# Expert stage with stationary weights: up weights loaded per tile, gate weights copied per tile, four gather buffers

## The reference, cut to what matters

```python
E, K, H, F, R = (8, 2, 256, 512, 64)             # experts, chosen per token, width, hidden, rank
# x: 32 sequences of 64 steps, 256 wide = 2048 tokens
# 1 a gated recurrence over the 64 steps, 32 sequences at once
gate = sigmoid(h @ Wh.T + z_t @ Wz.T + b);  h = tanh(h * leak + gate * z_t)
# 2 a mixture of experts on its outputs
gate_hidden = einsum('nh,erh->ner', x, W_A)
scores = sqrt(sum(gate_hidden * gate_hidden, axis=-1))          # top 2 of 8, softmax of the two scores
g  = einsum('ner,efr->nef', gate_hidden, W_B)
up = einsum('nh,efh->nef', x, W_up)
y  = einsum('nef,ehf->neh', silu(g) * up, W_down)               # weighted by the two softmax weights
# 3 x = x + that; a second recurrence h = tanh(x_t @ Wx + b + h @ Wh); a quantised feed-forward; x = x + that
```

## Time and profile before

| | |
|---|---|
| median of 3 runs | 414.03 us (411.77 to 414.64) |
| profiled execution | 413.37 us |
| its span, first to last instruction | 411.6 us |
| PE, DVE, ACT, POOL busy, share of the span | 81%, 64%, 56%, 54% |
| stage A, expert stage, stage C, about | 0 to 129, 129 to 296, 296 to 411 us |

### The profile page before, as it was taken

The page is one execution under the profiler, slowest core; times in us unless marked ns, Lnnn a source line. Parts: engine busy times, 40 slices in busy tenths (PEclk is TensorE's granted clock), DMA queues, the critical chain, the costliest instruction groups (busy, mean ns, idle before and its releaser), DMA issues.

```text
span 411.6 us, 11966 instructions
## 1 busy us (share of the span) xinstructions
PE 332.1 (81%) x3816; PEld 229.1 (56%) x3817; DVE 265.0 (64%) x910; ACT 231.2 (56%) x730; POOL 223.1 (54%) x219
## 2 busy tenths in 40 slices
PE   2677777767836999899999798999947978888984
PEld 1444444444523667567666565666745756666852
DVE  6545565578844896685866686535345767768884
ACT  2356665655634554455554464455435766767982
POOL 5569999998973353545445455542033545454220
PEclk9999999996986999999999999999985899999999
DMA  8991357531231467522222232232221122121001
GB/s 220 231 369 41 100 221 280 203 118 40 78 96 32 150 177 210 167 84 76 70 82 74 72 86 70 70 77 51 66 65 53 28 66 66 51 76 51 29 27 52
DMA packets 24922, 42.97 MB, mean 104 GB/s; under 512 B 4066, under 2 KB 17762, under 8 KB 23988
## 3 DMA queue, kind: packets, MB, share of 16 engines
q1 hardware_dynamic: 19120, 23.50, 18.1%
q0 software_dynamic: 5488, 18.98, 15.8%
q10 hardware_dynamic: 276, 0.01, 0.0%
HBM read 28.97 MB, written 13.50 MB: 103 GB/s over the span
## 4 chain that ended last, share of the span: by engine, by line
PE 46%; another core or an unknown queue 8%; ACT 8%; DVE 5%; issue 3%; DMA 2%; POOL 1%; ACTq 0%; DVEq 0%; SPq 0%; POOLq 0%
PE bank L1036 12%; PE bank L1012 9%; PE bank L1024 4%; PE bank L999 3%; PE bank L830 3%; PE bank L1143 3%; PE bank L837 3%; PE bank L1173 2%; ACT z_hi L748 2%; PE bank L1107 2%; PE bank L990 1%; DMA gs<-gate_rows,row_of_slot 1%; ACT wrec L760 1%; PE bank L992 1%
## 5 line engine op out<-in xcount | busy, mean ns | idle before, releaser
L830 PE MATMUL bank<-h_hi,wrec_hi 128*128 128x32 f16 x512 | 43.9, 181 | 44.0 <-ACT h_hi L636 26.0
L830 PEld LDWEIGHTS bank<-h_hi,wrec_hi 128*128 128x128 f16 x512 | 34.0, 98 | 72.8 <-ACT h_hi L636 46.7
L536 POOL DMA_INDIRECT xs<-hs_rows,row_of_slot x37 | 35.2, 950 | 71.7 <-PE bank L992 58.3
L1036 PE MATMUL bank<-wdn_s,wrec 128*128 x468 | 59.9, 275 | 4.8 <-ACT wrec L678 3.7
L1012 PE MATMUL bank<-wup_s,xt 128*128 x234 | 62.9, 379 | 0.0
L1568 DVE TENSOR_TENSOR wrec<-bank,wrec 128x512 f16<-128x512 f32 x39 | 26.9, 690 | 47.7 <-ACT wrec L678 41.1
L1036 PEld LDWEIGHTS bank<-wdn_s,wrec 128*128 128x128 f16 x468 | 43.5, 97 | 24.3 <-issue 11.8
L560 POOL DMA_INDIRECT z_lo<-y_rows,slot_i x32 | 32.5, 1014 | 30.6 <-DVE stage L1682 16.0
L1298 DVE TENSOR_TENSOR_SCAN bank<-bank,terms 128x128 f32<-128x128 f32 x64 | 27.6, 431 | 27.7 <-ACT bank L632 25.8
L539 POOL DMA_INDIRECT gs<-gate_rows,row_of_slot x39 | 37.5, 961 | 11.9 <-issue 11.9
L672 ACT ACTIVATE z_lo<-bank 128x256 f32<-128x256 f32 x39 | 14.9, 383 | 49.7 <-PE bank L1036 37.3
(11 more groups left out here) (261 smaller groups left out, 969.1 us busy)
## 6 DMA issues: line engine op xcount, KB each, us to landing
y_rows<-z_lo SPq DMA_DIRECT2D x39, 128.0 KB
stage<-wup POOLq DMA_DIRECT2D x2, 2048.0 KB, 10.8
gate_rows<-ga_s SPq DMA_DIRECT2D x16, 256.0 KB, 3.2
stage<-wdn POOLq DMA_DIRECT2D x2, 2048.0 KB, 10.2
stage<-wb SPq DMA_DIRECT2D x2, 1024.0 KB, 13.2
hs_rows<-hs_out SPq DMA_DIRECT2D x16, 128.0 KB, 2.6
stage<-w SPq DMA_DIRECT2D x4, 512.0 KB
stage<-x_tm SPq DMA_DIRECT2D x4, 512.0 KB
```

The lines of the kernel that those rows point to most:

```text
L536: pool.indirect_dma_start(out=xs[par][:, :], out_offset=None, in_=hs_dram[0:tokens, :], in_offset=bass.IndirectOffsetOnAxis(ap=row_of_slot ...
L830: mm(fm(par)[:, ft, cols], w[:, m, kt, fcols], h_hi[pp][:, kt, pcols], start=False, stop=True, skip_group_check=True)
L1036: ins = mm(bank[6][:, 0:D], act_t[:, a, ft, :], w_slice(wdn_s, b, ft, e), start=n == 0, stop=n == len(todo) - 1)
```

## The change

- PE: in gate and up the weights become the stationary operand and the tokens move, in blocks of 128: gate has 8 matmuls of 128 columns (four of them over 64 rows), up has 24. The result comes out with the hidden dimension on partitions, so `transposed_act` is gone, and ACT and DVE split the activation straight from SBUF.
- The stationary weights lie at fixed places. Up: stage A writes the split weights to `expert_rows` in memory (`keep_weights`, four DMAs of 1 MB in 1 KB pieces, in SP's list behind tiles 6 to 9), and SP loads 512 KB per tile into one of four buffers that take the place of the high half of `wup_s`. Gate: ACT copies 128 by 512 f16 per tile (`gate_weights`); for tiles 0 and 1 SP copies them by DMA.
- Gate rows are stored twice side by side (512 B a row), by two DMAs whose pieces are 256 B; a gather brings 512 B. POOL's gathers have four buffers throughout and wait for the transposes of tile j-4.
- The two `split_rec` stand behind gathers 16 and 18. ACT stores the result of tile j-2 instead of j-1. Stage C's loads are 16 parts of 256 KB. The loops over tiles of PE and SP take four tiles at a time.

```diff
-    ga_dram = nc.dram_tensor("gate_rows", (NTOK * E, R), F32, kind="Internal").ap()
+    ga_dram = nc.dram_tensor("gate_rows", (NTOK * E, 2 * R), F32, kind="Internal").ap()
+    w_dram = nc.dram_tensor("expert_rows", (E * P, EXPERT_ROW), F16, kind="Internal").ap()
...
# SP
                 sp.wait_ge(ga_out, tile + 1)
-                sp.dma_start(ga_dram[bass.ds(tile * P * E, P * E), :].rearrange("(p e) c -> p (e c)", e=E),
-                             ga_s[par][:, :]).then_inc(ga_st[par], 16)
+                for c in range(2):
+                    sp.dma_start(ga_dram[bass.ds(tile * P * E, P * E), c * R:(c + 1) * R].rearrange("(p e) c -> p e c", e=E),
+                                 ga_s[par][:, :].rearrange("p (e c) -> p e c", e=E)).then_inc(ga_st[par], 16)
+            def keep_weights(n):
+                sp.wait_ge(w_split, n // 2 + 1)
+                kt, a = n // 2, n % 2
+                at = (a * KT + kt) * F
+                sp.dma_start(w_to[:, :, at:at + F], wup_s[:, a, kt]).then_inc(w_kept, 16)
+            def load_weights(j, b, of=None):
+                if live(j - 4, STILES):
+                    sp.wait_ge(u_mm, j - 3)
+                e = expert_of(j, of)
+                sp.dma_start(w_now[b], w_dram[bass.ds(e * P, P), :]).then_inc(w_here[b], 16)
+                return e
+            sp.wait_ge(w_kept, 16 * 4)
+            sp.wait_ge(s_word, 1)
+            for j in range(2):
+                e = load_weights(j, j)
+                sp.dma_start(gate_now[j][:, :], wb_s[:, bass.ds(e, 1), :].rearrange("p a f -> p (a f)")).then_inc(gate_first, 16)
+            store_gates(TILES - 2, 0)
+            load_weights(2, 2)
...
+            for j in range(16):
+                load_weights(j + 4, j % 4, min(j + 4, FIRST - 3) if j + 4 < FIRST else None)
                 store_y(j, j % 4)
                 load_part(j)
...
# POOL
-                    pool.wait_ge(xt_mm, (j - 3, j - 1)[j >= 6])
+                    pool.wait_ge(xt_mm, j - 3)
...
# ACT
+            def gate_weights(j, par):
+                sc.reg_load(word_reg, word_i[0:1, bass.ds(of, 1)])
+                e = sc.snap((packed >> 3 * (c + 1)) & (E - 1), min_val=0, max_val=E - 1)
+                sc.wait_ge(g_mm, j - 1)
+                sc.activation(gate_now[par][:, :], wb_s[:, bass.ds(e, 1), :].rearrange("p a f -> p (a f)"), ACT.Copy
+                              ).then_inc(gate_here, 1)
             def expert_tile(j, q):
                     silu_of(j, par)
+                    gate_weights(j + 2, par)
                     act_high(j - 1, 1 - par)
+                    store_tile(j - 2, (q - 2) % 4)
                     copy_in(j + 2, par)
-                    store_tile(j - 1, (q - 1) % 4)
...
# PE
-                ins = mm(bank[2][:, :], gh_s[par][:, :],
-                         wb_s[:, part, bass.ds(e, 1), :].rearrange("p a n -> p (a n)"), start=part == 0, stop=part == 1)
+            for f in range(FT):
+                mm(bank[2][:, block_of(f)], gate_now[par][:, block_of(f)], gh_s[par][:, :],
+                   start=f == 0, stop=False, skip_group_check=True)
+                ins = mm(bank[2][:, block_of(f)], gate_now[par][0:R, block_of(f)], gl_s[par][:, :],
+                         start=False, stop=True, skip_group_check=True)
...
+            for f in range(FT):
+                for n, (a, c) in enumerate(parts):
+                    ins = mm(bank[4 + par][:, block_of(f)], up_now[b][:, a, kt, block_of(f)], xt[par][:, c, kt, :], ...)
-            def transposed_act(j, par):
...
# DVE
-                ve.tensor_tensor(act_t[:, 1, :, :]..., bank[(7, 3)[par]][:, :], act_t[:, 0, :, :]..., ALU.subtract)
+                ve.tensor_tensor(act_t[par][:, 1, :, :]..., act[par][:, :], act_t[par][:, 0, :, :]..., ALU.subtract)
```

More of the change, by code:

```diff
@@ L36 @@
 ROUND = 1536.0
+EXPERT_ROW = 2 * KT * F
 def live(t, count=TILES):
@@ L104, in adaln_ffn @@
         wa_s = sb("wa_s", [P, 2, KT, E * R], F16)
-        wb_s = sb("wb_s", [P, 2, E, F], F16)
+        wb_s = sb("wb_s", [P, E, F], F16)
+        gate_now = [sb(f"gate_now{i}", [P, F], F16) for i in range(2)]
         wup_s = sb("wup_s", [P, 2, KT, E, F], F16)
@@ L171, in adaln_ffn @@
         x1t = free_w[:, 2 * F + 2 * D:2 * F + 3 * D].bitcast(F16).rearrange("p (a k t) -> p a k t", a=2, k=KT)
+        w_flat = wup_s[:, :, :, :, :].rearrange("p a k e f -> p (a k e f)")
+        w_now = [w_flat[:, b * EXPERT_ROW:(b + 1) * EXPERT_ROW] for b in range(4)]
+        up_now = [x.rearrange("p (a k f) -> p a k f", a=2, k=KT) for x in w_now]
         peak = sb("peak", [P, 4])
@@ L298, in adaln_ffn @@
         act_r = sem("act_r")
-        at_mm = sem("at_mm")
+        w_split = sem("w_split")
+        w_kept = sem("w_kept")
+        w_here = [sem(f"w_here{i}") for i in range(4)]
+        gate_first = sem("gate_first")
+        gate_here = sem("gate_here")
         at_hi_r = sem("at_hi_r")
@@ L383, in _ @@
+            w_to = w_dram.rearrange("(e p) n -> p e n", p=P)
+            def keep_weights(n):
[3 more added lines that the diff above has]
+                sp.dma_start(w_to[:, :, at:at + F], wup_s[:, a, kt]).then_inc(w_kept, 16)
             store_rows(0, 0)
-            with sp.Fori(0, (TILES - 2) // 2) as i:
+            for i in range((TILES - 2) // 2):
                 store_rows(2 * i + 1, 1)
                 store_gates(2 * i, 0)
+                if 3 <= i < 5:
+                    keep_weights(2 * i - 6)
@@ L497, in _ @@
             pool.wait_ge(s_stage[1], 32)
-            then_wait(split(wb_s[:, 0], wb_s[:, 1], stage[1][:, :].rearrange("p (e f) -> p e f", e=E)))
+            wb_f = stage[1][:, :].rearrange("p (e f) -> p e f", e=E)
+            then_wait(high(wb_s[:, :, :], wb_f))
+            then_wait(pool.tensor_tensor(wb_s[R:P, :, :], wb_f[R:P, :, :], wb_s[R:P, :, :], ALU.subtract))
             load_staged(3)
@@ L687, in copy_in @@
                               ).then_inc(xt_ready, 1)
-                sc.activation(gh_s[par][0:R, :], bank[0][0:R, 2 * P:3 * P], ACT.Copy).then_inc(gh_ready, 1)
+                sc.activation(gh_s[par][:, :], bank[0][:, 2 * P:3 * P], ACT.Copy).then_inc(gh_ready, 1)
             def silu_of(j, par):
@@ L740, in _ @@
             act_high(STILES - 1, 0)
+            store_tile(STILES - 2, (STILES - 2) % 4)
             def gelu(t, par, half):
@@ L1096, in _ @@
                        ).then_inc(position_mm, 1)
-            with pe.Fori(7, (STILES - 5) // 2) as i:
-                expert = experts()
-                expert_tile(2 * i + 3, 1, expert, 0)
-                expert_tile(2 * i + 4, 0, expert, 1, 2 * i + 5)
+            with pe.Fori(4, (STILES - 3) // 4) as i:
+                for q in (1, 3):
+                    expert = experts()
+                    expert_tile(4 * i + q, q, expert, 0)
+                    expert_tile(4 * i + q + 1, q + 1, expert, 1, 4 * i + q + 2)
             def x1_transposed(t, par):
@@ L1185, in tanh_tile @@
                     if isinstance(k, int) and (k, s) == (0, 0):
-                        down(STILES - 1, expert(1))
+                        down(STILES - 1, 0, expert(1))
                     if s == 0:
```

179 lines of the change are left out of this document (93 added, 86 removed).

## The result

The changed kernel is slower: 449.9 us (median, 447.0 to 450.8) against 413.2 us of the kernel before, run beside it, a ratio of 1.089 with a 95% interval of 1.085 to 1.094. Forecast were 397 us and a range up to 409. The profiled execution has a span of 449.0 us; stage A is as long as before, stage C within 2 us, and the whole loss lies in the expert stage.

A forecast was written before the change was run, and what follows sets the result against it. PE's columns were taken to set the expert stage's pace, with DVE a second bound in tiles 1 to 7. Terms -0.2 - 3.1 - 12.0 - 3.4 + 2.0 = -16.7 took 413.4 to 396.7, 397 against the median; forecast 391 to 401, range 387 to 409.

The forecast's parts named there:

- Transposes gone: Expert stage, PE: the f32 transposes of the activation fall away, saving 0.43 us of PE per tile.
- Gate and up in blocks: Expert stage, PE: 32 load and matmul pairs of 128 columns at 55 ns, 1.76 us against 1.73, +0.03 a tile.
- pace of the pairs: Rival, gate and up of every tile: at 98 ns a pair +54 us, so 450; chance 0.05.
- the columns stay: Gate and up on PE: the same 4096 columns as before, so the lower bound on added cost was nothing.
- The rule weighed there: Gate and up: about 81 ns per 128-column matmul in sustained pairs, 0.8 us more a tile, about 429 us.
- The gathers run four tiles ahead, which covers a late landing: Expert stage transfers: gathers issued early hide late landings; only tile 11's gather, in a fuller queue, was priced, +1 us.
- Tiles 0 to 9: Early expert stage: DVE's 25.3 us from tile 0's to tile 6's split becomes 22.2, giving -3.1 us.
- tiles 9 to 38: Rest of the expert stage: 30 tiles at 0.40 us less each, -12.0 us.
- late high halves: Expert stage, before down: ACT's high half comes about 1 us ahead, removing two thirds of 5.2 us short waits, -3.4.
- Start of the expert stage: Two weight loads and two gate copies land in time; without stage A's 5.7 us pause, about 2 us late.
- Stage A, ACT's copy, SP's list at nothing: Stage A's extra transfers and ACT's gate copy cost nothing; SP's waits there are already met; its expert-stage jitter shared +1 us.
- crowded stage A: Rival, stage A: 256 B gate pieces above 35 ns make stores late; 408 us at 41 ns; chance 0.06 beyond 44 ns.

The follow-up runs named there:

- e1: Changed kernel with the low gate product made over 128 rows, the lower 64 zero, instead of 64; on the quicker chip 375.3 us, ratio 0.999.
- e13: The kernel before, unchanged, traced again in a later batch: 412.3 us.
- e10: e7 with POOL's old wait, for the transposes of tile j-2 instead of j-4: 411.9 us, ratio 0.996 to the kernel before.
- e9: The kernel before with the run-ahead alone: four gather buffers throughout, POOL waiting for the transposes of tile j-4: 431.6 us, ratio 1.047.
- e18: The kernel before with a small POOL memset, not waited for, behind every indirect DMA: 407.0 us, ratio 0.986.
- e8: e1 with gate rows stored and gathered once, other half zero, so the product with the low gate weights is left out: 423.5 us, ratio 1.023.
- e6: The changed kernel, unchanged, run again in batch two on a chip of the 413 us: 446.9 us, ratio 1.078 to the kernel before.
- e7: e1 with the gate copies of tiles 0 and 1 issued earlier, behind the row store of tile 14: 425.4 us, ratio 1.028.
- e12: e7 again, unchanged, as the base of batch three: 425.1 us, ratio 1.030 to the kernel before.
- e11: e7 with weight loads of 128 rows of 128 B instead of 512 KB from tile 11 on, leaving out part of the computation: 425.9 us, ratio 1.031.

## Why the prediction was wrong

**Transposes gone, -0.43 a tile:** right; with equal shapes the tile is 3.44 us (e1), forecast 3.41.

**Gate and up in blocks, 55 ns a pair:** the step that failed. It held for up (56 ns) and was applied to the gate product too, whose matmuls alternate between 128 and 64 rows; the row behind it had only 128. Measured 160 ns, +0.84 us a tile: 4.27 instead of 3.41, and 3.44 in e1 where the shapes are equal. In time 21.5 us, on both kinds of chip. The rival "pace of the pairs" had the sign and the time (450), and decides from 68 ns on, but by luck: it put 98 ns on all 32 pairs, while up has 56 and the gate product 160, and over a third of the loss is the run-ahead's. Its reason, the pairs, is refuted by up. I spoke there of "the columns stay" and priced the 64 rows nowhere. The rule weighed there, from the Trainium skill's "TensorE: Matmul & The Clock Gate", section "Back-to-back issue gap", does not hold for up: 56 ns over 24 pairs.

**"The gathers run four tiles ahead, which covers a late landing":** priced at nothing, and the second failure. On the quicker chip the sentence holds (7.7 us for it). On the other three the run-ahead costs 13.2 us here and 19 in the kernel before. The cue stood in the rows: three long ACT waits of "something the profile doesn't show". I kept them as a constant and did not ask what POOL did beside them. It issued runs of gathers, which the old wait at L534 kept short. POOL and then ACT of the kernel before, at the second of the three:

```profile
251.30 0.94 POOL L536 DMA_INDIRECT xs<-hs_rows,row_of_slot  x1 [1.60 <-PE bank L992]
252.55 0.94 POOL L539 DMA_INDIRECT gs<-gate_rows,row_of_slot  x1 [0.30 <-issue]
253.79 0.95 POOL L560 DMA_INDIRECT z_lo<-y_rows,slot_i  x1 [0.30 <-issue]
...
255.61 0.60 ACT L678 ACTIVATE wrec<-bank 128x512 f16<-128x512 f32 x1 [2.41 <-remote]
```

And where POOL has no wait between the gathers even there, at the end of stage A (eight from 113.9 to 122.8 us), ACT stops for 5.9 us: the pause that the prediction left as it was.

**Tiles 0 to 9, -3.1; tiles 9 to 38, -12.0; late high halves, -3.4:** two thirds of the first came, the rest not. (The -3.1 itself adds the 0.2 us of the moved POOL split where it should take it off; worked out rightly it is -3.5.) In the traces of e13 (before) and e10 (both causes taken out; two of the three like chips), tile 1 to tile 11 takes 129.4 to 169.1 and 131.2 to 168.8: -2.1. Tile 11 to 38 takes 114.0 and 116.9 us: +2.9, although tiles without a wait are at 3.44. Behind tile 38 it is 127.4 and 123.8. What remains in e10 is this, PE from 168 to 286 us, waits in total, times, longest; e13 ahead of it:

```profile
PE bank L999 <- ACT terms L696: 5.3, 3, 1.9
PE bank L1036 <- issue: 1.3, 2, 0.9
```

```profile
PE bank L1113 <- DVE wrec L1642: 3.6, 1, 3.6
PE bank L1100 <- issue: 3.1, 8, 1.1
PE bank L1113 <- issue: 2.9, 6, 0.7
```

PE itself now stops without a named reason in 15 places, 6.2 us, where it was 2 places and 1.3 us (and 5.3 by way of ACT); it issues 1334 matmuls in this stretch instead of 818, and its clock is 0.97 instead of 1.00. Over 27 tiles at pace, 92.9 us, e10 loses 24.0, e13 over 102.9 loses 11.1. Waits of PE are 12.9 and 7.5 of these; of the rest the clock is about 3.5 us in e10, an estimate from 0.03 x 116.9.

The 3.6 us in the list have a cause of their own, which the prediction priced only as engine time. DVE stood still for a part of stage C's weights:

```profile
173.24 0.69 DVE L1642 TENSOR_TENSOR wrec<-terms,wrec 128x512 f16<-128x512 f32 x1 [3.91 <-DMA stage<-w]
```

Cut into 256 KB and set behind twice as many stores, the last of these weights is issued at 169.17 us; as four parts of 512 KB it was at 151.08 (e13), and DVE of e10 needs it at 169.3. Every trace with the change has this wait of DVE, 3.0 to 8.8 us, no trace of the kernel before, e9 or e18 has it. PE pays 3.6 us for it in e10 and 1.8 in e1. No run puts the loads back, so its worth in time was not measured.

On the quicker chip e1 takes 99.8 us for these 27 tiles, 6.9 over 27 x 3.44, loses 6.5 us at the start to the gate copies, and is level with the kernel before. No trace of the kernel before exists from that chip, so where its 376.6 us lie stays open.

**Start of the expert stage, "about 2 us late" if stage A's pause were gone:** the mechanism was right, the size wrong: 6.5 us on the quicker chip, since both copies stand behind a load of 512 KB and PE waits for both. With the pause the wait is 0.7 us.

**Stage A, ACT's copy, SP's list at nothing:** right. The copy takes 0.63 us and no wait follows it. The "crowded stage A" did not come, though the DMA engines are at 97% from 50 to 100 us (63.3% and 33.8% for the two queues): ACT waited for a gate store once in all of stage A, 1.2 us, and e8 shows no price. The first queue's 63.3% are 506 us of engine time; less 168 for the kept weights and 37 for seven row stores that leaves 301 for 14336 pieces of 256 B, 21 ns each (an estimate from this row and the earlier trace rows), the figure that the forecast took. (At twice that the rival there would cost 13 us, not 11.)

In sum, on the chips of the 413 us: alternation +21.5, run-ahead +13.2, and -0.6 for all the rest, where -16.7 was forecast, make +34.1; e6 measured +33.3, the first runs +36.8. The match with e6 proves little: the differences chain into one another, and it only says that e7 and e12 lie alike above the kernel before (+11.9 and +12.6). Why the first runs lose 3.4 us more is open.

What stays open is why a run of gathers stops the other engines, and only on some chips. A reading that offers itself is that their instructions come late: the engines stop at any instruction. The Trainium skill, "Runtime: NRT & Kernel Launch", section "Instruction fetch mechanics", states that each sequencer fetches its code in blocks by a DMA queue of its own; such queues are in the profile (25 and 18 packets in the changed kernel). The third crawl speaks against this reading. The DMA queues of the changed kernel from 262.5 to 333 us:

```profile
q1 hardware_dynamic: 4003, 8.37, 36.9%
q0 software_dynamic: 919, 2.30, 12.6%
```

Neither instruction queue moved a packet in these 70 us, and yet PE, ACT and DVE crawl from 284 to 294 us; no fetch of these queues ended there that they could have waited for. So the cause stays open, with this reading the less likely one.

## What to carry to other kernels

Price a matmul run by a row with the same sequence of shapes: a change between 64 and 128 rows costs 0.1 us each time; zero padding takes it away, grouping three quarters of it. Waits of an engine that nothing in the profile explains are no constant; look for what runs beside all of them, here POOL's indirect DMAs in a row, before loosening what spaces it. When loads are cut smaller and set behind more stores, check when the last one is needed, not only what they cost. A wait that looks like mere lateness may be what keeps a burst short: try the looser wait alone (e9) first.

## What the runs showed of the hardware that I had not expected

- Eight 128-column matmuls in turn over 128 and 64 rows start 160 ns apart, the same grouped in two fours 81 ns on average, all over 128 rows 56 ns; every record says 0.22 to 0.23 us.
- A run of eight indirect DMAs of POOL, 1.25 us apart, makes PE, ACT and DVE crawl for 6 to 10 us on three of four chips, with the weight loads beside it or nearly without them (e12, e11); a pair every 3.55 us does it far less (14.7 us gained), a pair every 2.78 us nearly as much (2.8 gained). No packet of an instruction queue moves during the third of the crawls. One chip shows nothing of it, and there the kernel before takes 376.6 instead of 413 us.
- In and after a crawl TensorE's granted clock is down: 0.64 over 174.5 to 192 us, 0.74 over 240 to 260 us. The 24 matmuls of up that took 1.50 us take 2.77 there (190.02 and 254.88).
